# Four-layer gated transformer kernel: half of the routed experts' low weight halves made on GpSimd instead of VectorE

## The reference

```
x = x + tanh(g_xattn[i]) * xattn_i(layernorm(x), ctx)
x = x + tanh(g_ffn[i])   * ffn_i(layernorm(x))
```

```
probs = softmax(x @ gate_w + gate_b);  top 2 of 8 experts per token, at most 320 tokens an expert
for each expert e:  h = relu(x[idx_e] @ w1[e] + b1[e])        # 256 -> 1024
                    y[idx_e] += weight * (h @ w2[e] + b2[e])  # 1024 -> 256
```

## Time and profile before

| | |
|---|---|
| median of 3 runs | 2273.85 us |
| profiled execution | 2259.13 us, of which span 2257.4 us |
| TensorE matmul / weight load busy | 1962.2 us (87%) / 1654.7 us (73%) |
| VectorE busy | 1198.8 us (53%), 1944 instructions |
| ScalarE busy | 800.8 us (35%) |
| GpSimd busy | 531.4 us (24%), 412 instructions |
| L1542 (VectorE, wlo) | 112 instructions, 136.3 us |
| L1511 (VectorE, wlo, first expert) | 12 instructions, 13.9 us |

### The profile page before, as it was taken

How to read it: one execution, slowest core, us unless ns; L and a number is a source line. 1 busy time by engine, 2 the same in 40 slices (tenths; PEclk the granted TensorE clock), 3 DMA queues, 4 the chain that set the end, 5 groups by cost and what they waited for, 6 DMA issues and landing times.

```text
span 2257.4 us, 30730 instructions
## 1 busy us (share of the span) xinstructions
PE 1962.2 (87%) x10206; PEld 1654.7 (73%) x10206; DVE 1198.8 (53%) x1944; ACT 800.8 (35%) x1428; POOL 531.4 (24%) x412
## 2 busy tenths in 40 slices
PE   4637996796999999999999999999965995895894
PEld 2337996685888888888888888888744995685894
DVE  6875775666344443344443444443445665665564
ACT  2116885342222222222222222222222772332572
POOL 5012332425022221022222022220001231430341
PEclk8858998998999999999999999999966998996897
DMA  6025663101000000000000000100013441102453
GB/s 222 0 66 160 206 193 98 33 0 56 0 28 28 28 28 10 18 28 28 28 28 14 14 28 28 46 0 0 0 40 111 144 140 54 47 0 75 134 169 124
DMA packets 98834, 138.58 MB, mean 61 GB/s; under 512 B 14564, under 2 KB 78310, under 8 KB 98400
## 3 DMA queue, kind: packets, MB, share of 16 engines
q1 hardware_dynamic: 91232, 121.69, 16.9%
q0 software_dynamic: 7552, 16.24, 2.6%
HBM read 117.22 MB, written 24.90 MB: 63 GB/s over the span
## 4 chain that ended last, share of the span: by engine, by line
PE 70%; DVE 12%; issue 10%; POOL 3%; ACT 3%; DMA 2%; DVEq 0%; POOLq 0%; ACTq 0%; SPq 0%
PE ps L566 66%; POOL sc L478 2%; PE ps L577 2%; DVE lnx L1192 1%; POOL xs L474 1%; DVE bn L1199 1%; ACT whi L1088 1%; DVE q_den L1247 1%; DVE xs L1571 1%; ACT ps L1103 1%; DVE wlo L1542 1%; PE ps L835 1%; PE ps L876 1%; DVE q_relu L1240 1%; DVE h_lo L1523 0%
## 5 line engine op out<-in xcount | busy, mean ns | idle before, releaser
L566 PE MATMUL ps<-xTh,whi 128*128 (+4 forms) x1520 | 566.8, 373 | 9.6 <-DVE xTl L1519 5.5
L566 PE MATMUL ps<-xTl,whi 128*128 (+4 forms) x1520 | 558.2, 367 | 0.0
L566 PE MATMUL ps<-xTh,wlo 128*128 (+4 forms) x1520 | 558.0, 367 | 0.0
L1362 DVE TENSOR_TENSOR h<-h_act,ps 128x512 f32<-128x512 f32 x256 | 176.2, 688 | 630.2 <-ACT h_act L1062 630.2
L1062 ACT ACTIVATE h_act<-ps 128x512 f32<-128x512 f32 x256 | 153.3, 599 | 790.6 <-PE ps L566 790.6
L566 PE MATMUL ps<-h_hi,whi 128*128 128x512 f32 (+3 forms) x1008 | 353.0, 350 | 0.6 <-DVE h_lo L1366 0.6
L566 PE MATMUL ps<-h_hi,wlo 128*128 128x512 f32 (+3 forms) x1008 | 352.8, 350 | 0.0
L566 PE MATMUL ps<-h_lo,whi 128*128 128x512 f32 (+3 forms) x1008 | 352.8, 350 | 0.0
L566 PEld LDWEIGHTS ps<-xTh,whi 128*128 128x128 f32 x1520 | 288.5, 190 | 64.1 <-DVE h_lo L1523 7.6
L566 PEld LDWEIGHTS ps<-xTl,whi 128*128 128x128 f32 x1520 | 288.7, 190 | 47.0
L566 PEld LDWEIGHTS ps<-xTh,wlo 128*128 128x128 f32 x1520 | 288.2, 190 | 47.0
(11 more groups left out here) (248 smaller groups left out, 2174.8 us busy)
## 6 DMA issues: line engine op xcount, KB each, us to landing
wraw<-in_L_w SPq DMA_DIRECT2D x124, 512.0 KB, 3.4
wraw<-in_L_ffn_Wg SPq DMA_DIRECT2D x16, 512.0 KB, 3.9
wraw<-in_L_ffn_Wu SPq DMA_DIRECT2D x16, 512.0 KB, 3.9
wraw<-in_L_ffn_Wd SPq DMA_DIRECT2D x16, 512.0 KB
y_tok<-wraw SPq DMA_DIRECT2D x3, 2048.0 KB, 11.5
x_tok<-lnx SPq DMA_DIRECT2D x12, 512.0 KB, 4.0
lnx<-y_tok SPq DMA_DIRECT2D x12, 512.0 KB, 5.9
wat<-in_attn SPq DMA_DIRECT2D x16, 256.0 KB, 5.8
```

The source lines that it names most:

```text
L566: return pe.matmul(out_, lhsT, rhs, start=start, stop=stop)
L1362: dve.tensor_tensor(h_32[:, f % 2, :], h_act[:, f % 2, :], ps[:, (f % 2) * 2 + 1, :], ALU.mult).then_inc(f_h, 1)
```

## The change

Of the four pieces of each routed expert VectorE makes the first and the third, GpSimd the second and the fourth, for the first expert of a stage as for the rest. `w_lo` stays one counter, so whoever makes a piece now waits for `w_lo` to have reached the piece before it. On GpSimd the second piece stands between gather(e+2) and scatter(e-1), the fourth behind scatter(e-1).

```diff
-LOW_ON_VECTOR = {0: True, 2: True, 3: True}
+LOW_ON_VECTOR = (0, 2)
+LOW_ON_POOL = (1, 3)
@@ gpsimd, moe
                 def lower(u, q):
                     pool.wait_ge(w_hi, PIECES[name] + 4 * u + q + 1)
+                    pool.wait_ge(w_lo, PRIMED + PIECES[name] + 4 * u + q)
                     pool.tensor_tensor(wlo[:, u % 2, q, :], wraw[:, q, :], whi[:, u % 2, q, :].bitcast(F32), ALU.subtract).then_inc(w_lo, 1)
...
-                if on_pool:
-                    for q in range(4):
-                        lower(0, q)
+                for q in LOW_ON_POOL:
+                    lower(0, q)
...
                 for e in range(items):
-                    low = on_pool and e + 1 < items
-                    if low:
-                        lower(e + 1, 0)
                     if e + 2 < items:
                         gather(e + 2)
-                    if low:
+                    if e + 1 < items:
                         lower(e + 1, 1)
-                        lower(e + 1, 2)
                     if e > 0:
                         scatter(e - 1)
-                    if low:
+                    if e + 1 < items:
                         lower(e + 1, 3)
                 scatter(items - 1)
@@ vector, moe
-                if LOW_ON_VECTOR[layer]:
-                    for q in range(4):
+                if LOW_ON_VECTOR:
+                    for q in LOW_ON_VECTOR:
                         dve.wait_ge(w_hi, PIECES[name] + q + 1)
+                        dve.wait_ge(w_lo, PRIMED + PIECES[name] + q)
                         dve.tensor_tensor(wlo[:, 0, q, :], wraw[:, q, :], whi[:, 0, q, :].bitcast(F32), ALU.subtract).then_inc(w_lo, 1)
...
                 def weights_lower(u, s, q):
                     dve.wait_ge(w_hi, PIECES[name] + 4 * u + q + 1)
+                    dve.wait_ge(w_lo, PRIMED + PIECES[name] + 4 * u + q)
                     dve.tensor_tensor(wlo[:, s, q, :], wraw[:, q, :], whi[:, s, q, :].bitcast(F32), ALU.subtract).then_inc(w_lo, 1)
...
                     for f in range(FC):
                         lower(e, f)
-                        if LOW_ON_VECTOR[layer] and f % 2 == 1 and not end:
+                        if f % 2 == 1 and f // 2 in LOW_ON_VECTOR and not end:
                             weights_lower(e + 1, 1 - s, f // 2)
```

More of the change, by code:

```diff
@@ L497, in moe @@
                 name = f"ffn{layer}"
-                nth, items, tiles, on_pool = MOE.index(layer), ITEMS[layer], IR[layer] // P, not LOW_ON_VECTOR[layer]
+                nth, items, tiles = MOE.index(layer), ITEMS[layer], IR[layer] // P
                 def lower(u, q):
                     pool.wait_ge(w_hi, PIECES[name] + 4 * u + q + 1)
+                    pool.wait_ge(w_lo, PRIMED + PIECES[name] + 4 * u + q)
                     pool.tensor_tensor(wlo[:, u % 2, q, :], wraw[:, q, :], whi[:, u % 2, q, :].bitcast(F32), ALU.subtract).then_inc(w_lo, 1)
```

## The result

| | kernel before | kernel after |
|---|---|---|
| median of 20 runs each | 2270.18 us (2263.93 to 2274.20) | 2276.42 us (2270.91 to 2280.89) |
| profiled execution / its span | 2259.13 / 2257.4 us | 2278.31 / 2276.5 us |
| VectorE busy | 1198.8 us | 1130.6 us, 1882 instructions |
| GpSimd busy | 531.4 us | 680.7 us, 474 instructions |

The ratio after / before is 1.0026, 95% interval 1.0015 to 1.0038: slower by 6 us and less than the 0.5% that I had set as the bound. I had forecast slower, 2293 us with a range of 2278 to 2312. The spans of the two profiled executions differ by 19.1 us; the sum had said 19.4.

The account below looks back on a forecast made before the run. TensorE was taken to set the pace. New waits of 14.3 us in ffn0 and 5.1 us in ffn3, all else 0, made 19.4 us, added to the median of 2273.85 for 2293 us, range 2278 to 2312.

Parts of the forecast that it names:

- What bounds the kernel now, part (a): TensorE sets the pace, losing 0.19 us at chunk 2, alike at 6; taking VectorE's second and fourth pieces gains 0.
- (b): 62 subtractions added to GpSimd in the routed stages, at 2.398 us each as in ffn1.
- (c), ffn0: One-counter wait: VectorE's first next piece waits for GpSimd's fourth, 1.19 us at each of 12 experts, 14.3 us.
- (c), ffn3: GpSimd's loop closes at 16.55 us against a period of 15.38: +1.17 for experts 2 to 6, 5.1 us after slack.
- (c), ffn2: Wait of 0.3 us covered by TensorE's slack, GpSimd's loop of 16.55 under the period of 17.96: 0.
- (d): First expert of a stage: 5.1 us where pieces took 4.63, hidden behind VectorE's wait for the router: 0.
- (e): Other queues: SyncE's weight reloads, later gathers and matmuls reading the fourth piece all still come in time: 0.
- (f): GpSimd's subtraction doesn't slow VectorE in routed stages: its steps read PSUM, and the counter orders the pieces: 0.
- The rule on descriptor writing: Skill page's claim that tensor_tensor doesn't hold up descriptor writing; forecast disagreed, adding 0.65 us in the loops.
- Bounds: Whole change: low 8 us, high 29 us (ffn0 18.6, ffn3 10.3), so 2282 to 2303 on the median.
- 1 to 4: GpSimd early enough, 0.16; load gain wins, 2268, 0.04; loop binds everywhere, 2317, 0.12; VectorE's PSUM steps held up, 2349, 0.02.
- rival 1: GpSimd's fourth piece is ready early enough: 2283 with half the delay, 2274 with none; chance 0.16.

Follow-up runs that it names:

- u1: The kernel before, unchanged, run again for its profile: median 2264.4 us, ffn0 periods 13.96 and 12.64 in turn.
- s1: The kernel before, unchanged, run again: 2264.1 us, ratio 0.9998 to the kernel before.
- v2 to v4: Kernel before with ffn0 loops changed: TensorE's over four experts; TensorE's written out (ratio 1.0000); ScalarE's and VectorE's over four. Periods 12.85 to 13.01 us.
- w3: The kernel before with TensorE's ffn0 loop over four experts in a pass instead of two: periods even, no time given.
- t3: Mirror image of the kernel after: GpSimd makes the first and third pieces, VectorE the second and fourth: 2249.1 us, ratio 0.9960 to the kernel before.
- t1: The kernel after with VectorE's and GpSimd's pieces counted by two semaphores, neither waiting for the other's: ratio 1.0093 to the kernel before.
- w2: The kernel after, unchanged, run again: median 2276.7 us, ratio 1.0085 to the kernel before.

## Why the prediction was wrong

All groups side by side; "form" is that of the ffn0 periods in the profile of the kernel before taken in that group:

| group | form | before, us | after, us | ratio |
|---|---|---|---|---|
| the result | not profiled in that group | 2270.2 | 2276.4 | 1.0026 |
| s | 13.98 / 12.66 | 2264.9 | 2274.4 | 1.0053 |
| u | 13.96 / 12.64 | 2264.4 | 2272.8 | 1.0043 |
| w | even, 12.87 | 2258.3 | 2276.7 | 1.0085 |
| t | even, 12.87 | 2257.9 | | |
| v | even, 12.87 | 2257.1 | | |

The kernel after stays within 4 us; what moves is the kernel before, by 13.

**The step that failed** is the last of the sum: "That execution stands 14.7 below the median of the runs, 2273.85; on the median 2273.85 + 19.4 gives 2293". The execution with the profile was of the even form, and the sum is right for that: 19.4 forecast, 16.9 by the periods of the two traces, 18.4 (15.8 to 22.6 by the interval) measured in group w. The 14.7 us above it were not a constant that both kernels carry. In groups s and u 5 to 6 us of it are a stall in front of chunk 4 in every second expert (u1: 5.2 us in ffn0 and 0.9 in ffn2, by the sums of its periods against the even ones; s1: 5.2 and 0.2; 6.9 between the medians of the two kinds of group), which the kernel after doesn't have: it pays the new wait and is rid of the stall. 16.9 - 6.1 = 10.8, measured in group u 9.7 by the ratio and 8.4 between the medians; 16.9 - 5.4 = 11.5 in group s, measured in the same two ways 12.0 and 9.5. The remainder, from 2264.6 to the 2270.2 of the result, is lacking in the kernel after too, but no execution of the kernel before with it was profiled. That it is more of the same stall is my guess and not shown. Nor is the cause of the stall shown: in a group all profiles of kernels with ffn0 unsplit were of one form, one and the same chip had both (groups s and t), and the loops of v2 to v4 and w3 ran in even groups. The sum's 19.4 against the 19.1 between the two spans is partly luck: 16.9 stand in the loops, and 2.2 outside them.

By the steps:

- *What bounds the kernel now, part (a)*: right, and t3 shows it by its reverse. The two gaps stood behind the first and third pieces; rid of them, the period falls by 0.55 us (12.87 to a mean of 12.32), where I had 2 x 0.2, having read only the late start of one matmul and not that of the next (266.86).
- *(b)*: right, 2.40 us each.
- *(c), ffn0*: mechanism and place right, +1.00 per expert where I had 1.19. The hand-over from scatter to subtraction is 0.03 us (266.45 + 1.00 to 267.48), not 0.2, and from subtraction to VectorE 0.03, not 0.08. Term 12.2 for 14.3.
- *(c), ffn3*: right, the loop is 16.38 for 16.55, 4.7 us for 5.1. Two errors cancel: hand-overs shorter, but the gather row beside VectorE's piece takes 2.01 for 1.02, so +1.0 and not +0.65.
- *(c), ffn2*: right, 17.96 in both.
- *(d), (e)*: right. The router's first step still waits 11.66 us (12.06 before), and no reload shows up late.
- *(f)*: right for the change as made, since L1521 stays at 0.42 us for 128x256. The hold-up that it describes is the reason for which t1, without the counter, is no better.
- *The rule on descriptor writing*: the gather row at 270.04 ends 0.91 us after VectorE's piece (269.91 + 1.23), at 272.05. It takes 2.01 us for 1.02, so it is held up for 0.99 of the 1.10 us that it shares with a tensor_tensor with two SBUF inputs. The Trainium skill's page "SBUF — State Buffer" (section "Who interferes with whom") says that tensor_tensor doesn't stall DMA issued this way; the measurement decides. The indirect DMA also reads its row numbers (`x_idx`) from SBUF; whether that read is what waits isn't shown.
- *Bounds*: the high one of ffn0 adds up to +8.13, not 8.17, so 18.1 and not 18.6 us; that changes nothing.
- *Rivals*: 1 to 4 didn't come, by the traces. The median, +6 us, lies just under the +8 to +10 of rival 1 with half the delay, but not for its reason: GpSimd was not early enough. The real rival was missing from the list: the change takes away a stall that the profiled execution happens not to have. The gap between profile and median that I had noted was the sign that the two differ.

VectorE's own two pieces of the first expert and the router's first step in ffn0, from its timeline after:

```profile
141.69 1.23 DVE L1509 TENSOR_TENSOR wlo<-wraw,whi 128x1024 fp32r<-128x1024 f32 x1
145.50 1.23 DVE L1509 TENSOR_TENSOR wlo<-wraw,whi 128x1024 fp32r<-128x1024 f32 x1 [2.59 <-POOL wlo L505]
158.39 0.29 DVE L1443 TENSOR_TENSOR r_p<-ps,rb 128x128 f32<-128x128 f32 x1 [11.66 <-PE ps L563]
```

## What to carry to other kernels

Before work is moved off an engine, look for the instruction that stands in front of the bottleneck's gaps: of four equal pieces, two were worth 9 to 13 us when given away and the other two cost 6 to 18. When a helper engine takes a step that another waits for, put it ahead of the helper's DMA issues, not behind; one moved line gave back all of the loss but 1 us. And where a profiled execution stands well below the median of the runs, the difference may hold a stall that the change takes away: what a change costs on one trace can't simply be added to the median.

## Not expected of the hardware

- The same kernel has two forms of ffn0, even (12.87) and alternating (13.9 / 12.6), one or the other in all profiles of a group whose ffn0 is as before, 7 us apart in the median.
- Executions of one kernel also differ by when TensorE's clock rises. Of the 20 runs of the kernel after beside the result, nine took 2270.9 to 2273.1 us at a mean granted clock of 0.921 to 0.923, and ten 2276.7 to 2280.9 at 0.919 or 0.920 (the twentieth, 2276.1 at 0.921). The window of the stretch ahead of the loops of ffn0, the kernel after in its first trace; the granted clock, behind the engines, is 0.66, a mix of the levels 1.2 and 2.4 GHz:

```profile
137.00:213.00 76.00, 53.27 (x366) 51.46 (x367) 34.43 (x88) 29.63 (x55) 23.12 (x16) 0.66 0.39 127
```

The same in w2, at 0.76:

```profile
137.00:213.00 76.00, 53.10 (x419) 50.91 (x418) 37.11 (x92) 35.14 (x65) 29.95 (x19) 0.76 0.43 138
```

The busy time is the same 53 us, but w2 has done 419 matmuls for 366 and reaches its first `output` 7.6 us sooner (195.03 for 202.61). The spans are 2276.5 and 2269.3 with equal periods, so a single pair of traces can mislead by as much as this change costs.
- A subtraction on GpSimd can follow an indirect DMA in 0.03 us, while two indirect DMAs stand 0.30 apart.
